# Last part of the context's statistics, GpSimd's first weight splits and the first query staging moved to other stages of a four-layer latent-attention kernel

## The reference

```python
x = x + L0_xattn(ln(x), ctx)    # a1: causal self attention + MLP; a2: cross attention to ctx + MLP
x = x + L0_attn(ln(x)); x = x + L0_ffn(ln(x))      # rotary self attention; gated experts
x = x + L1_xattn(ln(x), ctx, ctx); x = x + L1_attn(ln(x)); x = x + L1_ffn(ln(x))
x = x + L2_xattn(ln(x), ctx); x = x + L2_attn(ln(x)); x = x + L2_ffn(ln(x))
x = x + L3_xattn(ln(x), ctx); x = x + L3_attn(ln(x)); x = x + L3_ffn(ln(x))
```

## Time and profile before

| | us |
|---|---|
| time before, median of 3 runs | 2217.67 (2217.34 to 2221.06) |
| the profiled execution's own time | 2217.62 |
| span of its trace, first to last instruction | 2215.9 |
| PE busy | 1993.9 (90%) |
| DVE busy | 1389.6 (63%) |
| ACT busy | 1148.2 (52%) |
| POOL busy | 594.8 (27%) |

### The profile page before, as it was taken

The page is one execution under the profiler, slowest core; times in us unless marked ns, Lnnn a source line. Parts: engine busy times, 40 slices in busy tenths (PEclk is TensorE's granted clock), DMA queues, the critical chain, the costliest instruction groups (busy, mean ns, idle before and its releaser), DMA issues. The chain is left out here.

```text
span 2215.9 us, 42645 instructions
## 1 busy us (share of the span) xinstructions
PE 1993.9 (90%) x14945; PEld 1718.6 (78%) x14945; DVE 1389.6 (63%) x2716; ACT 1148.2 (52%) x2326; POOL 594.8 (27%) x536
## 2 busy tenths in 40 slices
PE   5887999999887998489899999998898999998898
PEld 2666999999665885279599999966676998997677
DVE  8465777777546444741477777754456887885466
ACT  3245666666433442421466666642346877785254
POOL 2322222221011430100322222101334565650044
PEclk9797999999997998879999999999898999999999
DMA  6152100100012313422201001001317665651022
GB/s 238 34 239 109 46 32 31 46 30 0 5 63 110 151 55 140 195 82 92 87 31 46 31 30 37 9 1 29 108 53 171 162 163 142 160 143 36 19 81 78
DMA packets 49603, 183.66 MB, mean 83 GB/s; under 512 B 9392, under 2 KB 14896, under 8 KB 46128
## 3 DMA queue, kind: packets, MB, share of 16 engines
q1 hardware_dynamic: 47280, 179.03, 24.8%
q10 hardware_dynamic: 2176, 2.72, 0.5%
HBM read 125.72 MB, written 13.90 MB: 63 GB/s over the span
## 5 line engine op out<-in xcount | busy, mean ns | idle before, releaser
L622 PE MATMUL ps<-pTh,ch 128*128 128x256 f32 (+1 forms) x1248 | 379.6, 304 | 1.2 <-DVE pTl L1090 1.1
L1032 ACT ACTIVATE pTh<-ps 128x512 fp32r<-128x512 f32 (+1 forms) x512 | 236.2, 520 | 256.8 <-PE ps L932 256.6
L623 PE MATMUL ps<-pTl,ch 128*128 128x256 f32 (+1 forms) x1248 | 350.8, 281 | 0.0
L624 PE MATMUL ps<-pTh,cl 128*128 128x256 f32 (+1 forms) x1248 | 350.5, 281 | 0.0
L1090 DVE TENSOR_TENSOR pTl<-ps,pTh 128x512 fp32r<-128x512 f32 (+1 forms) x512 | 277.3, 583 | 83.7 <-ACT pTh L1032 83.1
L622 PEld LDWEIGHTS ps<-pTh,ch 128*128 128x128 f32 (+1 forms) x1248 | 237.6, 190 | 10.8 <-DVE pTl L1090 8.3
L623 PEld LDWEIGHTS ps<-pTl,ch 128*128 128x128 f32 (+1 forms) x1248 | 238.0, 191 | 0.0
L624 PEld LDWEIGHTS ps<-pTh,cl 128*128 128x128 f32 (+1 forms) x1248 | 236.9, 190 | 0.0
L622 PE MATMUL ps<-cTh,qh 128*128 128x512 f32 (+2 forms) x512 | 185.1, 362 | 14.6 <-POOL ql L886 9.8
L624 PE MATMUL ps<-cTh,ql 128*128 128x512 f32 (+2 forms) x512 | 179.8, 351 | 0.0
L623 PE MATMUL ps<-cTl,qh 128*128 128x512 f32 (+2 forms) x512 | 179.5, 351 | 0.0
(11 more groups left out here) (405 smaller groups left out, 4572.1 us busy)
## 6 DMA issues: line engine op xcount, KB each, us to landing
stacked<-weights SPq DMA_DIRECT2D x168, 100.2 KB, 2.2
stacked<-weights SPq DMA_DIRECT2D x168, 100.0 KB, 2.2
w<-l1f_w_in SPq DMA_DIRECT2D x16, 1024.0 KB, 9.2
wg<-l0f_guide_in SPq DMA_DIRECT2D x10, 704.0 KB, 5.6
z<-ctx_in SPq DMA_DIRECT2D x8, 832.0 KB, 12.9
z<-z SPq DMA_DIRECT2D x8, 832.0 KB, 10.0
keys<-ctx_in SPq DMA_DIRECT2D x8, 832.0 KB, 12.2
zT<-zT SPq DMA_DIRECT2D x8, 801.0 KB, 9.3
```

The lines of the kernel that those rows point to most:

```text
L622: pe.matmul(out, high, moving_high, start=start, stop=False)
L623: pe.matmul(out, high, moving_low, start=False, stop=False)
L624: return pe.matmul(out, low, moving_high, start=False, stop=stop)
L1032: nc.scalar.activation(pTh[0:w, PARTS[g][0]:PARTS[g][0] + n, slot, :], ps[0:w, turned_bank[slot][g], 0:n * P].rearrange("p (k r) -> p k r" ...
```

## The change

Three parts.

1. `statistics` ends after the second group. The third group's 39 `bn_stats` go into the first self attention as `aside`: 13 each after shift(1), shift(2) and shift(3), ahead of normal(0), normal(1) and normal(2); its `combine` goes ahead of normal(3). Its square root goes to ACT in the next block (`last_deviation`, at step 2 of `rows_to_norms`), its reciprocal to the start of `rows_on_vector`. The second group's square root on ACT moves from behind the third query product to behind the last key product (`n in (1, 11)` in place of `(1, 6, 11)`).
2. `first_split` runs on POOL in the `self_attention` block of l0a, l2a and l3a in place of the `rows_to_norms` block behind it.
3. The staging of the first four heads' queries goes from the start of `paired_attention` to POOL's part of the block in `paired_keys`, behind the split of the first keys; the counts of the semaphores `high_staged` and `staged` go down by one.

```diff
         def rows_to_norms(products, norms, turned, pool=None, landed=None, scalar=None):
...
+                        if step == per + 1 and scalar is not None:
+                            scalar(act)
                         if step >= per + 1:
                             keep_turned(act, step - per - 1, 4 + step - per - 1, turned, turned_ready)
...
+                    if pool_aside is not None:
+                        block.gpsimd(pool_aside)
+
...
                         for t in range(NT):
                             if t + 1 < NT:
                                 shift(t + 1)
+                            if aside is not None:
+                                aside(dve, t)
                             normal(t)
...
-                            pool.wait_ge(high_staged, c + 1)
+                            pool.wait_ge(high_staged, c)
...
-                            pool.wait_ge(staged, c + 1)
+                            pool.wait_ge(staged, c)
...
-                        stage(0, 0, 0, True)
                         loop_batches(pool, body)
...
-                            if u % 2 == 0:
-                                pe.wait_ge(staged, step * COUPLES + u // 2 + 1)
+                            if u % 2 == 0 and not (first and u == 0):
+                                pe.wait_ge(staged, step * COUPLES + u // 2)
...
-                        self_attention(qT, kT, v, oT, HP ** -0.5, HP, swapped, maskT=w("later"))
+                        self_attention(qT, kT, v, oT, HP ** -0.5, HP, swapped, maskT=w("later"), aside=context_z.last_statistics)
...
-                    moments(dve, 2, done)
-                    combine(dve, 2, done)
-                    invert(dve, 2)
+
+                def last_statistics(dve, t):
+                    group = GROUPS[-1]
+                    if t == 0:
+                        dve.wait_ge(landed[-1], 16 * len(group))
+                    if t == NT - 1:
+                        combine(dve, 2, done)
+                        return
+                    count = len(group) * KCH
+                    share = -(-count // (NT - 1))
+                    at = range(t * share, min(count, (t + 1) * share))
+                    for n in at:
+                        last = dve.bn_stats(stats[:, n, :], z[:, group[n // KCH], n % KCH, :])
+                    if at[-1] == count - 1:
+                        done(last)
...
-                    if n in (1, 6, 11):
-                        g = n // 5
-                        act.wait_ge(var_ready, g + 1)
-                        nc.scalar.activation(flat(dev, g), flat(dev, g), ACT.Sqrt).then_inc(std_ready, 1)
+                    if n in (1, 11):
+                        deviation_of(act, n // 10)
+
+                def last_deviation(act):
+                    deviation_of(act, 2)
...
                 def rows_on_vector(dve):
+                    invert(dve, 2)
                     dve.wait_ge(rdev_ready, len(GROUPS))
...
                 rows_to_norms(token_rows(oT, w.chunks("wo", KC), lambda t: plus(after[:, t, :], after[:, t, :])), norms,
-                              [(xT, None, None)], pool=first_split)
+                              [(xT, None, None)])
...
                             split(2, raw[:, 0:KEVEN], cTh[:], cTl[:])
+                            staged = qs[0:STACK, 0:2 * P].rearrange("p (h s) -> p h s", s=S)
+                            pool.wait_ge(taken_by_scalar, 1)
+                            pool.wait_ge(taken_by_vector, 1)
+                            pool.tensor_copy(staged, q[0:STACK, 0:4, 0:S]).then_inc(first_high, 1)
+                            pool.wait_ge(first_high, 1)
+                            pool.tensor_tensor(staged[32:64], q[32:64, 0:4, 0:S], staged[32:64].bitcast(F32), ALU.subtract)\
+                                .then_inc(first_staged, 1)
+                            pool.wait_ge(first_staged, 1)
```

More of the change, by code:

```diff
@@ L103 @@
                                   "raw_landed low_ready")
-ContextNormaliser = namedtuple("ContextNormaliser", "fetch statistics deviations first_rows second_rows "
+ContextNormaliser = namedtuple("ContextNormaliser", "fetch statistics deviations last_statistics last_deviation first_rows second_rows "
                                                     "vector_rows last_rows store_rows turn")
@@ L303, in keep_turned, with rows_to_norms @@
                                              bias=bias[:, c:c + 1], scale=scale[:, c:c + 1])
-        def rows_to_norms(products, norms, turned, pool=None, landed=None):
+        def rows_to_norms(products, norms, turned, pool=None, landed=None, scalar=None):
             per = len(norms)
@@ L2287, in two_attentions, with tail @@
         def two_attentions():
-            def tail(name, w, oT, norms, turned, first_pool=None, aside={}, last_pool=None):
+            def tail(name, w, oT, norms, turned, first_pool=None, first_scalar=None, aside={}, last_pool=None):
                 with ExitStack() as tmp:
@@ L2414, in invert @@
                     dve.reciprocal(flat(rdev, g), flat(dev, g)).then_inc(rdev_ready, 1)
+                done = Chain(nc.vector, chain)
                 def statistics(dve):
-                    done = Chain(dve, chain)
                     moments(dve, 0, done)
@@ L2423, in statistics, with deviation_of @@
                     invert(dve, 1)
-                    moments(dve, 2, done)
-                    combine(dve, 2, done)
-                    invert(dve, 2)
+                def last_statistics(dve, t):
[12 more added lines that the diff above has]
+                        done(last)
+                def deviation_of(act, g):
+                    act.wait_ge(var_ready, g + 1)
+                    nc.scalar.activation(flat(dev, g), flat(dev, g), ACT.Sqrt).then_inc(std_ready, 1)
                 def deviations(act, n):
-                    if n in (1, 6, 11):
-                        g = n // 5
-                        act.wait_ge(var_ready, g + 1)
-                        nc.scalar.activation(flat(dev, g), flat(dev, g), ACT.Sqrt).then_inc(std_ready, 1)
+                    if n in (1, 11):
+                        deviation_of(act, n // 10)
+                def last_deviation(act):
+                    deviation_of(act, 2)
                 def on_pool(b):
@@ L2525, in _ @@
                                                       gamma, beta, ALU.mult, ALU.add).then_inc(zT_dve, 1)
-                yield ContextNormaliser(fetch, statistics, deviations,
+                yield ContextNormaliser(fetch, statistics, deviations, last_statistics, last_deviation,
                                         lambda pool: rows_on_pool(pool, EARLY),
@@ L2561, in inner_attention @@
                     bias_on_pool(after, before, w(out_row))
-                    self_attention(qT, kT, v, oT, dh ** -0.5, dh, swapped, columns=w("bv") if biases else None)
+                    self_attention(qT, kT, v, oT, dh ** -0.5, dh, swapped, columns=w("bv") if biases else None,
+                                   pool_aside=first_split)
                 rows_to_norms(token_rows(oT, w.chunks("wo", KC), lambda t: plus(after[:, t, :], after[:, t, :])), norms,
-                              [(xT, None, None)], pool=first_split)
+                              [(xT, None, None)])
         def many_head_cross(name, dh, scale, row):
@@ L2613, in paired_keys @@
         def paired_keys(w, q, first_landed):
-            names = ("rows_landed", "product_ready", "taken_by_scalar", "taken_by_vector", "tile_high", "split_high", "split_low",
+            names = ("rows_landed", "product_ready", "first_high", "first_staged", "taken_by_scalar", "taken_by_vector", "tile_high", "split_high", "split_low",
                      "rows_high", "rows_low", "raw_landed", "low_ready") + tuple(f"pair_moved{p}" for p in range(H // 2))
-            with ExitStack() as own, signals(nc, *names) as                     (rows_landed, product_ready, taken_by_scalar, taken_by_vector, tile_high, split_high, split_low,
+            with ExitStack() as own, signals(nc, *names) as                     (rows_landed, product_ready, first_high, first_staged, taken_by_scalar, taken_by_vector, tile_high, split_high, split_low,
                      rows_high, rows_low, raw_landed, low_ready, *first_moved):
```

6 lines of the change are left out of this document (3 added, 3 removed).

## The result

The changed kernel takes 2204.13 us in the median of 7 runs (2197.75 to 2207.25), the kernel before 2217.67 (7 runs of the same set): 13.5 us less, ratio 0.9931, 95% interval 0.9913 to 0.9948.

The account below looks back on a forecast made before the run. TensorE is busy 90%, but the edits lie in short stages where it stands still, bounded by the engine that ends last. 5.6 + 3.0 + 0.4 + 1.4 = 10.4 us off 2217.62 gives 2207.2; 8-in-10 range 2203 to 2212.

Parts of the forecast that it names:

- The border: End of the first `dense` block: without the third group's statistics PE starts at 48.8 instead of 54.40, gain 5.6 us.
- The cover: a1's self attention: DVE's idle time ahead of `normal` hides three groups of 13 `bn_stats`, 2.52 us each; cost 0.
- l0a: Its norms block: three DVE operations are no longer held by POOL's splits, taking 0.48, 0.48 and 0.42 us; gain 3.0 us.
- l2a: Its norms block: a DVE scaling beside POOL's last split falls from 0.87 to 0.42 us; gain 0.4 us.
- The casts: Sign: POOL's casts begin about 2 us into the self attention, and DVE's subtraction beside them still takes 1.2 us.
- l3x: Its start: PE's first scores come 0.3 us after DVE's end, at 1685.0 against 1686.40; gain 1.4 us.
- statistics back: Rival, a1's self attention: `bn_stats` and masks slow each other; up to 7.6 us come back, 2214.8, half 2211.0; 10%.
- part 2 void: Rival, l0a's norms: the held operations cover a wait that comes anyway; 3.4 us shrink to nothing, 2210.6; 7%.
- POOL holds DVE: Rival, the three self attentions: POOL's splits hold DVE; parts of 15.7 us come back, 2222.9 at the whole; 3%.
- the clock stays up: Rival, first border: full clock holds through tile 0 of a1's self attention, saving some 3 us, 2204.2; 15%.
- The forecast as worked out, within 3 us on account of the clock: Whole kernel: the summed gain holds and the clock shifts it by up to 3 us, 2204 to 2210.5; 65%.
- the point: Whole kernel: the forecast time of 2207.2 us, 10.4 us below the profiled execution.

Follow-up runs that it names:

- `delay13`: The kernel before with 13 more `bn_stats` behind the third group's in the first `dense` block, adding 3.0 us: 2224.86 us, ratio 1.0030.
- `delay7`: The kernel before with 7 more `bn_stats` behind the third group's in the first `dense` block, adding 1.5 us: 2222.02 us, ratio 1.0020.
- the second: A second set of 6 runs of the changed kernel, unedited: 2206.94 us, ratio 0.9953 against the kernel before.
- Part 1 alone: The changed kernel with `first_split` and the staging put back, only the third group's statistics moved: 2214.54 us, ratio 0.9981 against the kernel before.
- part 3 alone: The changed kernel with the statistics and `first_split` put back, only the staging moved: 2217.64 us, ratio 0.9995 against the kernel before.
- the filler: Five unused PE transposes ahead of each `values(t)` in the self attentions of l0a, l2a and l3a, in the kernel before: 2216.97 us, ratio 0.9991.
- `split_twice`: The kernel before with POOL's first cast and subtraction done twice in the norms blocks of l0a, l2a and l3a: 2228.01 us, ratio 1.0048.

## Why the prediction was right or wrong

**Right: each term.** The border: PE at 48.83, forecast 48.8. The closeness is luck: by the clock in the products ahead it came at 47.9 to 49.3 us in other executions, a gain of 5.1 to 6.5 us, and the term had no such width. The cover: 1.33, 0.47 and 1.91 us of idle time left, forecast 1.3, 0.5 and 1.4 (the third was 0.5 us too low); the `bn_stats` took 2.60 us a group, not 2.52. l0a: 0.48, 0.48 and 0.42 us and a block 2.98 us shorter, forecast 3.0. l2a: 0.46, forecast 0.4. The casts begin 1.9 us into the self attention, and the subtraction keeps 1.2 us. l3x: the scores 0.32 us behind DVE's last. The three rivals that took a term away (statistics back, part 2 void, POOL holds DVE) each met a row against them. One detail was off at no cost: `combine` was to meet POOL's masks, but it ended at 76.80, as the mask began.

**Half right: "the clock stays up".** The clock was up at the border, as that rival said (first scores 0.91 us), and fell before tile 0's sums (1.88 us), so nothing like its 3 us came. The block behind the border took as long as before.

**Wrong: the size of the clock's share.** The step that failed is "The forecast as worked out, within 3 us on account of the clock", and the range's low end that followed, 2203. It priced the clock from one place, the stage whose gap changes, for one block and up to 3 us. The runs show it in many stages, short ones and the attention of l3x, behind an edit and ahead of it: one block can change by 5.3 us, what no edit explains by a balance of -3 us in the profiled execution and, in the delays, of +6.0 (`delay13`) and +11.8 us (`delay7`), and two executions of the same instructions differ by 3.1 us in their first 681. The miss is small beside that: 2202.4 against 2203, where the interval reaches from 2198.4 to 2206.1, and a first set like the second would have hit the point. By the mean clocks, the changed kernel had 0.0023 more than the kernel before, which by the slope is 3.0 us: the 13 runs' mean is 12.8 us below that of before, of which 9.8 are the change's. Part 1 alone, with a clock 0.0008 lower, had to give 1 us back, and part 3 alone lost 0.5 of its 1.1. The point would have stayed where it was, since the sign of this share could not be read from the trace of before; the range should have been some 5 us to each side of the sum, 2202 to 2212.

The Trainium skill ("TensorE: Matmul & The Clock Gate", section "HAM oscillation — how this bites in real kernels") lets the clock drop on long idle gaps. The trace disagrees in l0a: it fell to half at 667.2 with no gap of PE longer than 1.03 us since the block began, where the kernel before kept it up through gaps of up to 1.10 us.

**Open.** What decides which stage falls to half, and how much of it an edit's shift does and how much is the execution's own. The start of l0a's block doesn't decide it (653.61 gave 24.0 us, 653.53 and 653.70 gave 27.2). To part the two would take several profiled executions of one kernel. Whether the first set's 13.5 us or the second's 10.7 is nearer to the truth isn't settled either: their intervals overlap between 0.9937 and 0.9948, 11.5 to 14.0 us.

## What to carry to other kernels

Read an edit from the border that it moves: the engine that ends the block, the one that ends next, and the idle time that is to cover what is added; here that gave each part within 0.5 us in the profiled rows. Then ask what the border hangs on afterwards: here DVE's fixed work gave way to PE's, which goes with the clock. Widen the range for the granted clock by what the stages without an edit can do, a few microseconds of either sign for a kernel with this many of them, and look at the runs' mean clocks too, since a version that is 5 us faster may only have met a better pattern. Before a filler, a new order or an effect of a shift is believed, put it into the kernel before, and compare blocks that *nothing* has touched: here a block with a bare delay was 5.3 us longer, the same block without edit or delay was 2.1 us longer in another execution, and the filler did nothing.

## What the runs showed of the hardware

- The granted clock in l0a's self attention (matmuls of 32 to 128 rows, PE's idle gaps 1.1 us at most) falls to 0.50 or stays at 1.00 for the same instructions, and the stage takes 21.9, 24.0 or 27.2 us. Executions that differ in nothing ahead of it or in it gave 21.9 (before) and 24.0 us (`split_twice`).
- In the long attention of l3x the granted clock can fall to half for 3.4 us, as at 1858.4 and 2025.6 us before, or not at all, as in the changed kernel. The pair went with 2.9 us.
- DVE's operations between SBUF buffers are held to the end of POOL's (3.25 us instead of 0.42), `bn_stats` of SBUF rows aren't (7.58 us beside POOL's work on the context's rows, 7.57 alone), and those that read PSUM aren't (1.22 us).
